# Token statistics of six batches and the fill of the score operands moved to ScalarE in a kernel's opening

## The reference

```
_L0_attn_ref(x):
    v = x @ v_w
    pooled = x.mean(axis=1)                       # over a batch's tokens, (B, D)
    gl  = pooled @ gate_w + mod(pooled) . basis   # (B, H, M), H = M = 16
    wts = topk_sparse(gl, 8)
    arg = freqs . positions + phases ; kern_masks = sum(amps * sin(arg))
    kern = wts . kern_masks ; density = step(kern)
    scores = causal_kern(density)[i - j] + q_mod, k_mod terms (x @ cq_w, x @ ck_w)
    out = softmax(causal scores) @ v @ out_w ; LN ; FFN (gelu) ; LN
_L0_ffn_ref: silu(fp4_linear(x, w_gate)) * fp4_linear(x, w_up) -> fp4_linear(., w_down)
```

## Time and profile before

| | us |
|---|---|
| median of 3 runs | 1945.47 |
| lowest and highest | 1943.98, 1945.88 |
| profiled execution, its own time | 1947.52 |
| its span | 1945.7 |
| start of the loop on PE (L723) | 252.64 |
| one pass of the loop | 110.56 |

### The profile page before, as it was taken

One profiled execution on the slowest core, in us unless ns is written; L12 is line 12 of the kernel. 1 busy time (PEld: TensorE's weight loads), 2 busy tenths in 40 slices (PEclk: granted clock), 3 DMA queues, 4 the chain that ended last, 5 costly groups with the idle time before them and its releaser, 6 DMA issues.

```text
span 1945.7 us, 42571 instructions
## 1 busy us (share of the span) xinstructions
PE 1820.7 (94%) x12700; PEld 1311.4 (67%) x12700; DVE 1615.3 (83%) x5197; ACT 901.9 (46%) x1833; POOL 1103.7 (57%) x799
## 2 busy tenths in 40 slices
PE   8667999999999999999999999999999999999997
PEld 3234677676776767677776767677676767677766
DVE  7868879888898988888997988888897988889763
ACT  3024454454635445453545445463545445363542
POOL 3434746565664746465674756466574656566563
PEclk8777999999999999999999999999999999999999
DMA  5343223232223333232322323222332323322211
GB/s 170 117 123 89 64 74 108 65 105 73 77 74 83 108 73 95 65 103 70 93 76 73 107 75 95 73 82 71 99 90 73 107 62 103 77 78 74 63 56 33
DMA packets 138566, 165.35 MB, mean 85 GB/s; under 512 B 19758, under 2 KB 100655, under 8 KB 138453
## 3 DMA queue, kind: packets, MB, share of 16 engines
q1 hardware_dynamic: 138458, 164.30, 30.5%
...
## 4 chain that ended last, share of the span: by engine, by line
PE 60%; DVE 15%; issue 12%; POOL 6%; ACT 3%; DMA 3%; SPq 1%; DVEq 0%; ACTq 0%; POOLq 0%
PE ps L767 11%; PE ps L758 11%; PE ps L699 8%; PE ps L716 4%; PE ps L622 3%; PE ps L609 3%; PE ps L656 3%; PE ps L595 3%; POOL Pr L1174 3%; PE ps L672 2%; PE ps L731 2%; PE ps L652 2%; DVE st L956 2%; DVE nmax L1035 2%; DMA QS<-q_bias_parts 2%
## 5 line engine op out<-in xcount | busy, mean ns | idle before, releaser
L1174 POOL TENSOR_TENSOR Pr<-Pr,Tz 128x768 f32<-128x768 f32 (+2 forms) x384 | 478.2, 1275 | 248.5 <-ACT Pr L831 244.6
L1035 DVE CUSTOM_DVE_ANT_0 ps<-ps,future 128x512 f32<-128x512 f32 (+3 forms) x1024 | 474.6, 516 | 51.2 <-issue 50.9
L831 ACT ACTIVATE Pr<-ps 128x384 f32<-128x384 f32 x512 | 243.8, 489 | 352.7 <-PE ps L656 348.6
L622 PE MATMUL ps<-KS,QS 108*128 108x512 bf16 (+3 forms) x1024 | 218.3, 304 | 32.5 <-DVE nmax L1035 23.9
L758 PE MATMUL ps<-catT,w 128*128 128x256 f32 x1024 | 237.8, 380 | 0.7 <-ACT catT L894 0.7
L767 PE MATMUL ps<-w,gT 128*128 128x256 f32 x1024 | 232.9, 381 | 0.9 <-ACT gT L911 0.9
L1065 DVE SCALAR_TENSOR_TENSOR Pr<-ps,Tz 128x512 f32<-128x512 f32 x256 | 175.2, 684 | 54.7 <-ACT ps L820 46.7
L820 ACT ACTIVATE ps<-ps 128x512 f32<-128x512 f32 x256 | 150.4, 588 | 139.9 <-PE ps L652 138.4
L767 PEld LDWEIGHTS ps<-w,gT 128*128 128x128 f32 x1024 | 190.8, 190 | 25.7 <-ACT gT L911 1.3
L758 PEld LDWEIGHTS ps<-catT,w 128*128 128x128 f32 x1024 | 189.6, 190 | 26.3 <-ACT catT L894 0.9
L716 PE MATMUL ps<-wdT,hqT 128*128 128x256 f32 x768 | 178.0, 381 | 0.7 <-ACT hqT L870 0.7
...
## 6 DMA issues: line engine op xcount, KB each, us to landing
Tz<-kernel_rows SPq DMA_DIRECT2D x256, 256.0 KB, 3.5
...
```

Of the source, the lines that this page charges most:

```text
L622: ins = mm(o, QS[0:KROWS, 2 * p + e, it * P:(it + 1) * P], KS[0:KROWS, p, 0:n], start=True, stop=True)
L831: inc(af(Pr[:, p % 4, e, at:at + wd], src[:, 0:wd], ACT.Exp), "a_exp")
L1035: ins = v.tensor_tensor_reduce(o, o, future[:, S - n:S], -1.0, 3e38, ALU.add, ALU.min, nmax[:, 2 * pl + e, it:it + 1])
L1174: ins = g.tensor_tensor(a, a, Tz[:, p % 2, :, P * j:P * j + PAST[j]], ALU.mult)
```

## The change

Part by part, with the line numbers of the kernel before:

1. The two memsets of `KS` and `QS` leave POOL's step `ones`, and a new step `fill` on ACT writes the same values: two ACTIVATEs of 128x8x256 with bias 1.0 to `KS`, two of 128x2048 to `QS`. All four read a tile of zeros. `load.0` and SP's `ones` wait for a new semaphore `filled`; what is left of POOL's step (the memset of `v_new`) is moved up to stand behind the first `rs.0`.
2. For batches 5, 7, 9, 11, 13 and 15 ACT takes the statistics, with `accum_out`: four Copy over 128x256 give the sums of x, one 128x4 op turns them into minus the mean, four Square with that as bias give the sums of squares. DVE keeps one 128x4 op of each such `st`, and its `cp` reads the mean from the sums.
3. The head's order tables of all five engines are written anew. Loop and end are as before.

```diff
@@ pro:load.0 on SP, v of batch 0 on DVE, SP's ones
-                        sp.wait_ge(L["ready"], 3)
+                        sp.wait_ge(L["filled"], 2)
-                        dve.wait_ge(L["ready"], 3)
+                        dve.wait_ge(L["ready"], 1)
-                sp.wait_ge(L["ready"], 1)
+                sp.wait_ge(L["filled"], 1)
@@ def prologue_gpsimd, "ones"
-                g.memset(KS[:].rearrange("p q s -> p (q s)"), 1.0).then_inc(L["ready"], 1)
-                g.memset(QS[:].rearrange("p h s -> p (h s)").bitcast(F32), 0.0).then_inc(L["ready"], 1)
@@ DVE, "st"
+                if n in ACT_STATS:
+                    dve.wait_ge(L["rowsq"], ACT_STATS.index(n) + 1)
+                    v.tensor_scalar(p_ve[:, i, :], p_st[:, i, :, 2], 1.0 / D, EPS, ALU.mult, ALU.add).then_inc(L["var"], 1)
+                    return
@@ DVE, "cp"
-                v.tensor_copy(mean_all[:, T * n:T * (n + 1)], p_mv[:, i, :, 0])
+                if n in ACT_STATS:
+                    v.tensor_scalar(mean_all[:, T * n:T * (n + 1)], p_st[:, i, :, 0], 1.0 / D, None, ALU.mult)
+                else:
+                    v.tensor_copy(mean_all[:, T * n:T * (n + 1)], p_mv[:, i, :, 0])
@@ ACT, new steps; ACT_STATS = [5, 7, 9, 11, 13, 15], junk is a new tile
+            elif k == "st":
+                n = s[1]
+                i, m = n % NX, ACT_STATS.index(n)
+                act.wait_ge(x_sem[i], 16 * (n // NX + 1))
+                if n >= NX:
+                    act.wait_ge(L["mean"], n - NX + 1)
+                if m:
+                    act.wait_ge(L["rowsq"], m)
+                for t in range(T):
+                    ins = af(junk[:, t, :], x_in[i][:, t, :], ACT.Copy, accum_out=p_st[:, i, t, 0:1])
+                ins.then_inc(L["rowsum"], 1)
+                act.wait_ge(L["rowsum"], 2 * m + 1)
+                af(p_st[:, i, :, 1], p_st[:, i, :, 0], ACT.Copy, scale=-1.0 / D).then_inc(L["rowsum"], 1)
+                act.wait_ge(L["rowsum"], 2 * m + 2)
+                for t in range(T):
+                    ins = af(junk[:, t, :], x_in[i][:, t, :], ACT.Square, bias=p_st[:, i, t, 1:2], accum_out=p_st[:, i, t, 2:3])
+                ins.then_inc(L["rowsq"], 1)
+            elif k == "fill":
+                act.wait_ge(L["zero"], N_MEMSETS)
+                wide = zeros.unsqueeze(1).to_broadcast([P, PAIRS, zeros.shape[1]])
+                for i in range(S // zeros.shape[1]):
+                    at = slice(i * zeros.shape[1], (i + 1) * zeros.shape[1])
+                    ins = af(KS[:, :, at], wide, ACT.Copy, bias=1.0)
+                ins.then_inc(L["filled"], 1)
+                words = QS[:].rearrange("p h s -> p (h s)").bitcast(F32).rearrange("p (a n) -> p a n", n=zeros.shape[1])
+                for i in range(2):
+                    ins = af(words[:, PAIRS * i:PAIRS * (i + 1), :], wide, ACT.Copy)
+                ins.then_inc(L["filled"], 1)
@@ ORDER, head, ACT (a piece of the table; the rows below show what it does)
-            pre:rnd.13 pre:rnd.14 pre:rnd.15 pro:mT.0 pre:sin.8 pre:sin.9 pre:sin.10 pre:sin.11 pre:peak pre:sin.12
+            pre:st.7 pre:fill pre:st.9 pre:st.11 pre:st.13 pre:sin.7 pre:st.15 pre:peak pre:sin.8 pre:rnd.14
```

More of the change, by code:

```diff
@@ L75 @@
         sync="""
[L76 to L80, removed]
+            pre:px.0 pre:px.1 pre:waves pre:px.2 pro:xload pre:px.3 pre:ld.w_proj pre:ld.w_gate pre:ld.w_v
@@ L81 @@
+            pre:ld.basis pre:px.4 pre:ld.c0 pre:px.5 pre:px.6 pre:px.7 pre:ld.c1 pre:px.8 pre:px.9 pro:splitio
+            pre:ones pre:px.10 pro:load.0 pre:px.11 pre:px.12 pre:px.13 pre:px.14 pre:px.15 pre:rz pro:load.1
+            pre:ld.c2 pre:ld.w_rest pro:mio.0 first:xload pre:rows first:T.0 first:T.1 first:splitio first:T.2
+            first:T.3 first:mio.1 first:T.4 first:load.0 first:T.5 first:T.6 first:T.7 first:mio.0
         """,
         gpsimd="""
-            pre:iota pre:half pre:rs.0 pre:rs.1 pre:rs.2 pre:rs.3 pre:rs.4 pre:rs.5 pre:rs.6 pre:ones pro:projm.0
@@ L84 @@
[L84 to L88, removed]
+            pre:half pre:rs.0 pre:ones pre:iota pre:rs.1 pre:rs.2 pre:rs.3 pro:projm.0 pre:rs.4 pro:projm.1 pre:rs.5
@@ L96 @@
[L96 to L110, removed]
@@ L116 @@
[L116 to L130, removed]
@@ L131 @@
[L131 to L140, removed]
+            pre:sum.0 pre:arg.0 pre:arg.1 pre:arg.2 pre:sum.1 pre:arg.3 pre:arg.4 pre:arg.5 pre:arg.6 pre:arg.7
@@ new lines @@
+            pre:sum.13 pre:arg.14 pre:sum.14 pre:sum.15 pre:sum.16 pre:sum.17 first:mx.1.0.0 first:mx.1.0.1 pre:poolT
+            pre:mod pre:gl first:mx.1.0.2 first:mx.1.0.3 pro:mT.0 pre:wt.0 first:mx.1.0.4 pre:arg.15 pre:wide pre:kern
+            first:mx.1.1.0 first:mx.1.1.1 first:mx.1.1.2 first:mx.1.1.3 pre:wt.1 pre:wt.2 first:xT.0 first:xT.1
+            pre:wt.3 pre:wt.4 pre:wt.5 pre:wt.6 first:mx.1.1.4 pre:wt.7 pre:wt.8 first:proj.0 first:proj.1
+            first:sc.0.0 pro:xqT first:mx.1.2.0 first:mx.1.2.1 first:mx.1.2.2 first:mx.1.2.3 first:gu.0.0 first:proj.2
@@ L1293, in build @@
               "wtr", "wev", "arg", "mean", "rnd", "frac", "sin", "chain", "pe", "act", "kern", "tanh", "dens", "exp",
-              "rows", "ones", "ready", "pad", "half"]}
+              "rows", "ones", "ready", "filled", "pad", "half", "rowsum", "rowsq"]}
         x_sem = [L["x0"], L["x1"], L["x2"], L["x3"]]
@@ L1412, in prologue_vector @@
                     dve.wait_ge(L["scaled"], n - NX + 1)
+                if n in ACT_STATS:
+                    dve.wait_ge(L["rowsq"], ACT_STATS.index(n) + 1)
+                    v.tensor_scalar(p_ve[:, i, :], p_st[:, i, :, 2], 1.0 / D, EPS, ALU.mult, ALU.add).then_inc(L["var"], 1)
+                    return
+                k2 = 2 * sum(m not in ACT_STATS for m in range(n))
                 for t in range(T):
```

92 lines of the change are left out of this document (66 added, 26 removed).

## The result

| | before | changed |
|---|---|---|
| median us | 1945.68 | 2042.98 |
| runs | 4 (1943.98 to 1946.34) | 4 (2031.39 to 2045.79) |
| ratio, 95% interval | | 1.049 (1.0449 to 1.0532) |
| span of the profiled execution | 1945.7 | 2043.9 |
| start of the loop on PE | 252.64 | 247.14 |

The account below looks back on a forecast made before the run. Loop bound by PE and untouched, so only its start (252.64 us) shifts, DVE being busiest early in the head: +8 − 8 + 4.6 + 0 − 6.5 = −1.9 on 1945.47, some 1943.5 us; range 1936.5 to 1953.

Parts of the forecast that it names:

- the prediction's signs of being wrong: First maximum within 3 us of 70.22, ACT step over 4.3 us, or pooled to loop not 3 to 9 shorter.
- Theory B: From the experiments: new head hands the loop over in another phase, kept up by DVE and POOL blocking each other.
- DVE's stall at 31: Head: a small DVE copy of 7.41 us beside POOL's memsets; forecast to go with them, 7.3 us of DVE time.
- the third case: ACT becomes the bound: statistics steps at 4.9 us instead of 3.3, with separate accumulator reads; 1953 us, chance 0.21.
- from the first maximum to the last: Head: three of six statistics steps go to ACT, -5.7, and DVE idle time shrinks, -2.5; together -8 us.
- The third rival: Head: POOL's remaining operations still hold up small DVE operations, half the 7.3 us returns; 1950.5 us, chance 0.10.
- the relief of DVE: Head: statistics and stall off DVE, 18.7 us of its time; as rival, first maximum +2, 1937.6 us, chance 0.27.
- a later load: Head: load.0 issued at 62 to 71 instead of 62.39, behind the fill; first maximum +8 us.

Follow-up runs that it names:

- e2: Changed kernel with 6 do-nothing instructions (12 fulfilled waits) ahead of pooled on DVE; 1937.86 us, ratio to the kernel before 0.9961.
- e12: Changed kernel with four do-nothing instructions ahead of pooled on DVE; 1942.04 us, ratio to the kernel before 0.9968.
- e9: Changed kernel with GpSimd's FFN bias addition moved ahead of the score product in the loop; 1987.75 us, ratio to the kernel before 1.0217.
- e11: Changed kernel with three do-nothing instructions ahead of pooled on DVE; 2049.47 us, ratio to the kernel before 1.0534.
- e5: Changed kernel with 118 do-nothing instructions (236 fulfilled waits) ahead of pooled on DVE; 2012.7 us, ratio to the kernel before 1.0338.
- e1: Changed kernel with 49 do-nothing instructions (98 fulfilled waits) ahead of pooled on DVE; 1941.38 us, ratio to the kernel before 0.9974.
- e6: Changed kernel with 96 do-nothing instructions ahead of pooled on DVE; 1946.76 us, ratio to the kernel before 0.9997.
- e4: Changed kernel with 49 do-nothing instructions ahead of peak on ACT, DVE's stream left alone; 2041.47 us, ratio to the kernel before 1.0478.
- e8: Changed kernel with all statistics back on DVE, the rest, new orders included, as changed; 1950.08 us, ratio to the kernel before 1.0015.

## Why the prediction was wrong

**The step that failed** is the first one: "the loop is not touched: whatever the change is worth is the shift of the loop's start". The instructions of the loop are the same, and their place in DVE's stream is not. Six statistics steps of ten instructions became one each, 54 fewer, and with some waits that now stand by themselves DVE's head is 49 shorter. The loop's first four instructions are now the end of one piece of the stream. Three things follow. The first is shown apart by e2 and e12, which take the stall away; the second and the third go together in e9, and no run takes them apart:

1. The stall. The jump back comes behind L1124, which ends 1.0 us into a pass. The second piece is there 8.4 to 9.4 us into it, wherever the border lies: 9.0 and 9.4 in the changed kernel's second and third pass, 8.8 in e9, 9.2 in e11, 8.4 and 9.3 in the two passes of e5. In the kernel before, e1 and e6 DVE gets to that border later than this and nothing is seen. Against the second L1132 of a good pass (5.7) it is 3.7 us.
2. The meeting with GpSimd. L977 takes 2.55 us more beside the score product; e9 takes the meeting away and leaves the stall.
3. The clock. PE idles 3.5 us for L977 and then has a granted clock of 0.53 for 11 us, nearly all of it at the lower of the two levels, 1.2 GHz. In e9, where PE waits 1.0 us at most there, the pass keeps 1.00.

A late pass costs 6 to 10 us, of which e9 leaves 3.1 to 4.5, the stall alone. Thirteen passes, the first is spared: 103.7 us. No rival had this, and none of the prediction's signs of being wrong came true (first maximum at 82.28, an ACT step of 4.0, `pooled` to the loop 8.6 us shorter): all of them looked at the head. Theory B was wrong as a cause, but its mechanism is the second half of the loss. That the passes come out uneven (116.7 to 120.3) I did not take apart.

The Trainium skill, "Runtime: NRT & Kernel Launch", section "Instruction fetch mechanics", says that each engine reads its instructions through a small FIFO which is refilled in blocks, that prefetch is purely sequential, and that "A taken branch whose target isn't in the current 2-page window forces a DMA fetch of the target page before execution can continue". The runs agree with the mechanism (a packet right after the jump back and the next about 5 us later, no stall in the first pass). They disagree with the size: the page has blocks of 16 KiB, 256 instructions, while here a shift of 79 in one kernel did what -49 did in the other, and 118 moved the stall by 10 instructions the other way, so the pattern repeats after 128. By these shifts alone a divisor of 128, such as 64, would do as well; the five or six packets in a pass of 463 instructions speak for 128 to a packet, since pieces of 64 would need at least eight. The measurement decides, for DVE: another queue moved 21 instruction packets of 16 KB in the whole run, and the profile doesn't say for which engine.

```profile
q8 instruction: 21, 0.34, 0.1%
```

**The head**, point by point. These are places in one execution, and the head scatters: e9 has the changed kernel's head, e4 has it too up to `peak`, and `pooled` was at 118.63, 111.89 and 121.62 in the three, the start of the loop at 247.14, 241.67 and 251.62. So a difference of a few us in a place is no finding; the medians of the runs are the better guide.

| | forecast | changed kernel |
|---|---|---|
| DVE's stall at 31 | gone | gone |
| first norm | 22 | 22.13 |
| one ACT statistics step | 3.3 to 4 | 4.0 |
| fill ends | near 60 | 66.67 |
| `load.0` | 62 to 71 | 73.42 |
| first maximum | 78 | 82.28 |
| last maximum taken | near 107 | 105.2 |
| `pooled` | near 120 | 118.63 |
| `pooled` to the loop | 130.6 | 128.5 |
| start of the loop | 250.7 | 247.14 |

The ACT step has the separate read that the third case had for possible:

```profile
47.69 0.40 ACT L1625 ACTIVATE junk<-y 128x256 f32<-128x256 f32 x1
47.99 0.18 ACT L1625 ACTIVATION_READ_ACCUMULATOR junk<-y 128x1 f32 x1
...
59.37 3.69 ACT L1638 ACTIVATE KS<-ctxn 128x2048 bf16<-128x2048 f32 x2
...
83.51 0.42 ACT L1625 ACTIVATE junk<-catT 128x256 f32<-128x256 f32 x1 [12.89 <-DMA catT<-in_x]
```

but it overlaps with the next ACTIVATE, so a step stayed at 4.0 and ACT did not become the bound: it waits 12.89 us for batch 11. The fill ended later than forecast since ACT has hardly any idle time from 44.6 to 70.5. The term of the head that was mis-sized most is "from the first maximum to the last": 22.8 us in place of 36.9, so -14 and not -8. DVE is busy 19.4 of them, and the 8.5 us of idle time that it had the earlier trace rows have shrunk to 3.4:

```profile
82.28:105.10 22.82, 15.17 (x51) 4.54 (x52) 19.41 (x117) 13.77 (x53) 10.68 (x8) 0.73 0.63 176
```

The third rival, the stall in smaller pieces, did not come: one of DVE's small copies took 1.56 us (at 7.82), the other nine 0.17.

With the loop's place mended (e1, e2, e12) the kernel took 1937.9 to 1942.0, which is within the forecast range; that is no merit of its reasoning on the loop. e8 shows that the relief of DVE, which I had cancelled against a later load, is worth 9 to 12 us.
